# Bias rows written by ScalarE, dense spread of gamma and beta, and the last feed-forward pair by batch

## The reference

```python
# tokens: depthwise conv (3 taps) over time, linear 64 -> 128, biases, layernorm
x_sp    = conv(x, conv_w) + conv_b                 # per channel
x_mixed = einsum('btc,dc->btd', x_t, lin_w) + lin_b + emb.mean(axis=0)
h = (x_mixed - mu) * rsqrt(var + 1e-05) * ln_g + ln_b
# attention on n = layernorm(h): scores in 250 x 250 per batch, scale 1/8
V = softmax(Q K^T / 8) V0 ; the row c0 = argmin(row_sums of batch 0) is set to 0
h = h + V
# feed-forward over the 128 features, weights lower triangular
h = h + (gelu(layernorm(h) @ tril(W1).T + b1) @ tril(W2).T + b2)
```

## Time and profile before

| | us |
|---|---|
| median of three runs | 94.94 (94.71 to 95.37) |
| the profiled execution | 94.69 |
| its span in the trace | 92.9 |
| PE busy | 87.2, 94% of the span |
| DVE busy | 74.4, 80% |
| ACT busy | 69.3, 75% |
| POOL busy | 47.8, 51% |

### The profile page before, as it was taken

One profiled execution on the slowest core, in us unless ns is written; L12 is line 12 of the kernel. 1 busy time (PEld: TensorE's weight loads), 2 busy tenths in 40 slices (PEclk: granted clock), 3 DMA queues, 4 the chain that ended last, 5 costly groups with the idle time before them and its releaser, 6 DMA issues.

```text
span 92.9 us, 2013 instructions
## 1 busy us (share of the span) xinstructions
PE 87.2 (94%) x567; PEld 73.9 (80%) x567; DVE 74.4 (80%) x296; ACT 69.3 (75%) x215; POOL 47.8 (51%) x70
## 2 busy tenths in 40 slices
PE   4999699999999999999999999999999999999940
PEld 1356567789999999999999999999997877787840
DVE  3279997999698998869998895988989688793560
ACT  1666799899999969977889976697758983565200
POOL 7006398676554386539525519703996305791000
PEclk9999999999999999999999999999999999999999
DMA  2896000000000000000000000000000003036565
GB/s 17 213 280 212 0 0 4 4 0 0 7 0 0 0 0 0 7 4 0 0 4 4 0 7 0 0 0 0 0 0 7 0 0 110 0 110 169 162 175 167
DMA packets 3973, 3.86 MB, mean 42 GB/s; under 512 B 429, under 2 KB 3962, under 8 KB 3962
## 3 DMA queue, kind: packets, MB, share of 16 engines
q1 hardware_dynamic: 3610, 3.35, 12.8%
q10 hardware_dynamic: 352, 0.38, 1.5%
HBM read 1.68 MB, written 2.05 MB: 40 GB/s over the span
## 4 chain that ended last, share of the span: by engine, by line
PE 80%; DVE 9%; DMA 5%; issue 1%; SPq 0%; DVEq 0%
PE bank_o L483 15%; PE bank_s L458 15%; PE bank_at L470 8%; PE bank_pv L434 7%; PE bank_pv L443 7%; PE bank_s L518 7%; DMA x_all<-x_dram 5%; PE bank_x L366 4%; PE bank_x L496 4%; PE bank_nt L507 4%; PE bank_pv L507 4%; PE bank_nt L423 4%; DVE hb_all L1078 2%; DVE tap_a L994 1%; DVE xc L1000 1%; PE bank_o L366 1%
## 5 line engine op out<-in xcount | busy, mean ns | idle before, releaser
L483 PE MATMUL bank_o<-pv,at_sb 125*125 125x129 f32 x128 | 16.8, 273 | 0.0
L458 PE MATMUL bank_s<-n1t,pv 128*125 128x250 f32 x64 | 16.1, 374 | 0.0
L483 PEld LDWEIGHTS bank_o<-pv,at_sb 125*125 125x125 f32 x128 | 15.6, 187 | 0.1
L772 ACT ACTIVATE a<-bank_s,neg_max 125x250 f32<-125x250 f32 x32 | 13.4, 482 | 1.0 <-DVE neg_max L1039 1.0
L1039 DVE TENSOR_REDUCE neg_max<-bank_s 125x2 f32<-125x500 f32 x16 | 10.7, 668 | 2.2 <-PE bank_s L458 2.1
L458 PEld LDWEIGHTS bank_s<-n1t,pv 128*125 128x125 f32 x64 | 11.0, 187 | 0.9
L780 ACT ACTIVATE at_sb<-bank_at 125x500 f32<-125x500 f32 x16 | 9.6, 597 | 2.4 <-PE bank_at L470 1.8
L276 POOL TENSOR_TENSOR hb_all<-h_all,rows_sb 125x512 f32<-125x512 f32 x8 | 10.9, 1384 | 0.0
L765 ACT ACTIVATE pv<-bank_pv 128x508 f32<-128x508 f32 x15 | 9.0, 602 | 2.1 <-PE bank_pv L443 2.0
L272 POOL TENSOR_TENSOR h_all<-h_all,rows_sb 125x512 f32<-125x512 f32 x6 | 7.6, 1271 | 5.7 <-DVE h_all L1013 5.7
L1050 DVE SCALAR_TENSOR_TENSOR h_all<-bank_o,rinv_keep,h_all 125x128 f32<-125x128 f32 x32 | 9.8, 346 | 0.6
(11 more groups left out here) (137 smaller groups left out, 183.7 us busy)
## 6 DMA issues: line engine op xcount, KB each, us to landing
out_dram<-hb_all SPq DMA_DIRECT2D x7, 224.0 KB
x_all<-x_dram SPq DMA_DIRECT2D x8, 125.0 KB, 4.9
out_dram<-hb_all SPq DMA_DIRECT2D x2, 112.0 KB
w_sb<-weights_dram SPq DMA_DIRECT2D x1, 192.0 KB, 5.6
rows_sb<-rows_dram ACTq DMA_DIRECT2D x1, 187.5 KB
out_dram<-hb_all SPq DMA_DIRECT2D x6, 26.0 KB
tok_w<-tok_dram ACTq DMA_DIRECT2D x1, 130.0 KB, 3.1
w_sb<-weights_dram SPq DMA_DIRECT2D x1, 128.5 KB, 5.2
```

The source lines that it names most:

```text
L458: last = nc.tensor.matmul(s_ps[b % 2][:, a, :], p_sb(b)[:, a * H:(a + 1) * H], n1t[b % 2][:, :], start=True, stop=True)
L483: last = nc.tensor.matmul(o_ps[:, a, 0:DV], at_sb[:, c, a * H:(a + 1) * H], v_sb(b, c), start=(c == 0), stop=(c == 1))
L772: last = nc.scalar.activation(a_sb[b % 2][:, a, :], s_ps[b % 2][:, a, :], ACT.Exp, bias=neg_max[b % 2][:, a:a + 1])
```

## The change

It has five parts, and the lists of PE, ACT, DVE and POOL are written in a new order around them.

1. **Bias rows.** The bias row is formed on all 128 partitions (`bias_row`), ACT copies it to `cb_sb` (`out_cb`). For pairs 4 to 7 ACT writes it, four times side by side, into the PSUM bank (`write_bias`), and the linear layer is added to that. Pairs 2 and 3 still get it from PE as bfloat16 parts; the split is now four POOL instructions.
2. **gamma and beta.** One row of 1 KB is loaded into a zeroed tile, PE spreads it over 125 partitions (`spread_constants`, 256 columns), ACT copies it (`out_constants`). b2 is loaded and spread by a DMA of SP, behind all x pairs.
3. **First tap of pair 1** goes from DVE to ACT.
4. **Nine dummy matmuls become six.**
5. **Pair 7's feed-forward by batch.** Root, `normalize_2`, `turn_n2`, `out_n2t`, `up`, `gelu`, `down` and `finish` of pair 7 are two turns (j = 7 and 8) of one batch each.

```diff
+        def turn(j):
+            return (j, 0, 4, 2 * j + 2) if j < NP - 1 else (NP - 1, 2 * (j - NP + 1), 2, j + NP)
 @block.sync
...
+            sp.dma_start(b2_sb[:, :], rows[:, 2 * D:3 * D].broadcast_to((H, D))).then_inc(landed_b2, 16)
...
 @block.gpsimd
+            def split_hi():
+                pool.wait_ge(cb_out, 1)
+                pool.tensor_copy(cb_rows[:, :], cb_sb[:, :]).then_inc(cb_hi_ready, 1)
+            def split_rest():
+                pool.wait_ge(cb_hi_ready, 1)
+                pool.tensor_tensor(cb_rest[:, :], cb_sb[0:64, :], cb_rows[0:64, :], ALU.subtract).then_inc(cb_rest_ready, 1)
...
+            pool.memset(rows_raw[:, :], 0.0).then_inc(raw_zeroed, 1)
...
 @block.tensor
             def project_bias(k):
-                before = (0, 0, 1, 0, 4, 6, 10, 12)[k]
...
-                    pe.wait_ge(cb_ready, 3)
-                    if k >= 4:
-                        pe.wait_ge(conv_ready, k + 1)
-                    nc.tensor.matmul(dst, ones_b[:, :], cb_rows[:, :].unsqueeze(1).broadcast_to((C + 1, 4, D)),
+                    pe.wait_ge(cb_ready, 1)
+                    nc.tensor.matmul(dst, shares_b[:, :], cb_rows[:, :].unsqueeze(1).broadcast_to((128, 4, D)),
             def project_half(k, a):
                 pe.wait_ge(conv_ready, k + 1)
+                if k >= 4:
+                    pe.wait_ge(bias_ready, k - 3)
+            def spread_constants():
+                pe.wait_ge(mean_w_ready, 2)
+                pe.wait_ge(landed_rows, 16)
+                nc.tensor.matmul(bank_at[0:H, 0:2 * D], mean_w[:, 0:H], rows_raw[:, :], start=True, stop=True).then_inc(rows_mm, 1)
-            keep_warm(9)
+            keep_warm(6)
+            spread_constants()
...
 @block.scalar
...
-            act.dma_start(rows_sb[:, :], rows.broadcast_to((H, 3 * D))).then_inc(landed_rows, 16)
+            act.wait_ge(raw_zeroed, 1)
+            act.dma_start(rows_raw[0:1, :], rows[:, 0:2 * D]).then_inc(landed_rows, 16)
+            def out_constants():
+                act.wait_ge(rows_mm, 1)
+                nc.scalar.activation(rows_sb[:, :], bank_at[0:H, 0:2 * D], ACT.Copy, scale=float(C)).then_inc(rows_out, 1)
+            def out_cb():
+                act.wait_ge(cb_mm, 1)
+                nc.scalar.activation(cb_sb[:, :], bank_s[0][:, 0:D], ACT.Copy).then_inc(cb_out, 1)
+            def write_bias(k):
+                act.wait_ge(cb_out, 1)
+                act.wait_ge(conv_ready, k + 1)
+                nc.scalar.activation(x_bank(k)[0:H, :].rearrange("p (a d) -> p a d", d=D),
+                                     cb_sb[0:H, :].unsqueeze(1).broadcast_to((H, 4, D)), ACT.Copy).then_inc(bias_ready, 1)
+            out_constants()
+            first_tap(1)
+            first_tap(2)
             squares(0)
+            first_tap(3)
+            out_cb()
             squares(1)
...
```

More of the change, by code:

```diff
@@ L269, in add_beta, with split_low, add_b2 @@
+            def split_low():
+                pool.wait_ge(cb_mid_ready, 1)
+                pool.tensor_tensor(cb_rows[0:32, :], cb_rest[0:32, :], cb_rows[0:32, :], ALU.subtract)\
+                    .then_inc(cb_ready, 1)
             def add_beta(k):
-                pool.wait_ge(landed_rows, 16)
+                pool.wait_ge(rows_out, 1)
                 pool.wait_ge(x_scaled, 2 * k + 2)
                 pool.tensor_tensor(h_tiles[:, k, :, :], h_tiles[:, k, :, :], beta_4, ALU.add).then_inc(h_ready, 1)
-            def add_b2(k):
-                pool.wait_ge(resid_ready, 2 * k + 2)
-                pool.tensor_tensor(hb_all[:, k, :, :], h_tiles[:, k, :, :], b2_4, ALU.add).then_inc(hb_ready, 1)
+            def add_b2(j):
+                k, first, count, batches = turn(j)
+                tiles = slice(first, first + count)
+                pool.wait_ge(landed_b2, 16)
+                pool.wait_ge(resid_ready, batches)
+                pool.tensor_tensor(hb_all[:, k, tiles, :], h_tiles[:, k, tiles, :], b2_4[:, 0:count, :], ALU.add).then_inc(hb_ready, 1)
@@ L494, in turn_n2 @@
                     pe.wait_ge(n2t_ready, j - 1)
-                for n in range(4):
-                    last = nc.tensor.transpose(t2_ps[j % 2][:, n * H:(n + 1) * H], n2[:, j, n, :], ident[0:H, 0:H])
+                k, first, count, _ = turn(j)
+                for n in range(count):
+                    last = nc.tensor.transpose(t2_ps[j % 2][:, n * H:(n + 1) * H], n2[:, k, first + n, :], ident[0:H, 0:H])
                 last.then_inc(t2_mm, 1)
@@ L568, in _ @@
             queries(3)
+            values(3)
+            project_half(5, 0)
             turn_n1(4)
-            values(3)
+            project_half(5, 1)
             attend(0)
@@ L584, in _ @@
             turn_a(3)
+            turn_n1(7)
+            scores(5)
             queries(6)
-            scores(5)
-            project_bias(6)
             values(6)
-            turn_n1(7)
             attend(3)
             turn_a(4)
-            turn_n1(8)
             scores(6)
             queries(7)
+            values(7)
             project_half(6, 0)
-            values(7)
             project_half(6, 1)
+            turn_a(5)
+            turn_n1(8)
             attend(4)
-            turn_a(5)
             scores(7)
+            queries(8)
+            turn_a(6)
+            values(8)
             turn_n1(9)
-            queries(8)
-            values(8)
-            project_bias(7)
+            attend(5)
+            scores(8)
+            queries(9)
             project_half(7, 0)
+            values(9)
             project_half(7, 1)
-            scores(8)
-            attend(5)
-            turn_a(6)
-            queries(9)
             turn_n1(10)
-            values(9)
-            turn_a(7)
             attend(6)
             scores(9)
+            turn_a(7)
             queries(10)
@@ L782, in out_n2t @@
             def out_n2t(j):
+                k, first, count, _ = turn(j)
                 act.wait_ge(t2_mm, j + 1)
-                nc.scalar.activation(n2t[:, j, :], t2_ps[j % 2], ACT.Copy).then_inc(n2t_ready, 1)
+                nc.scalar.activation(n2t[:, k, first * H:(first + count) * H], t2_ps[j % 2][:, 0:count * H], ACT.Copy)\
+                    .then_inc(n2t_ready, 1)
             def gelu(j):
+                k, first, count, _ = turn(j)
                 act.wait_ge(f1_mm, j + 1)
-                nc.scalar.activation(g_sb[:, j, :], f1_ps[j % 2], ACT.Gelu, bias=b1_col).then_inc(gelu_ready, 1)
+                nc.scalar.activation(g_sb[:, k, first * H:(first + count) * H], f1_ps[j % 2][:, 0:count * H], ACT.Gelu, bias=b1_col)\
+                    .then_inc(gelu_ready, 1)
             act.wait_ge(landed_tok, 16)
@@ L816, in _ @@
             out_n1t(0)
+            out_qk(2)
+            squares(6)
             normalize_1(1)
-            spread_rows()
             out_p0()
             first_tap(4)
-            squares(6)
+            out_v0()
             out_n1t(1)
             squares(7)
-            out_v0()
+            spread_rows()
             normalize_1(2)
@@ L905, in _ @@
             out_at(12)
-            out_n2t(0)
+            gelu(0)
+            out_pv(15)
             exps(14)
-            out_pv(15)
             out_at(13)
```

474 lines of the change are left out of this document (228 added, 246 removed).

## The result

Six runs of the changed kernel have a median of 96.00 us, six of the kernel before 94.82; the ratio is 1.012 (95% interval 1.008 to 1.016). The change makes the kernel 1.1 us slower: outside the band of 1% around no change at the median, though the interval reaches into it. One run of the six took 98.6 us and is not in the ratio. The profiled execution took 95.98 (before: 94.69), its span is 94.1 (92.9).

What follows compares the result with a forecast made beforehand. PE was taken to bound the kernel, gapless from 13.50 to 88.26 us, behind a head chained over ACT, POOL and DVE. Terms 0.57 - 0.66 + 0.38 + 0.10 = +0.39 on 94.69 gave 95.1, range 93.7 to 96.6.

Steps and rivals of the forecast that it cites:

- the size of part 1: Bias rows of pairs 4 to 7: PE drops four matmuls, 1.06 us off its gapless stretch.
- the head eats it: Head through pair 4's halves: later queries and PE's waits for ACT cost +0.57, first bias row's 0.40 already taken off.
- nothing happens between 22 and 68 us: From pair 4's halves to the projections' end PE runs without gaps, three bias rows less: -0.66.
- The floor rival: Whole kernel: ACT keeps up and the head is not later; 93.7 to 94.1 us, chance 0.30.
- the order of Gelu and Exp, +0.38: Ahead of the transpose of batch 14's weights: ACT's table change back to Exp makes PE wait, +0.38.
- the third rival: First Gelus: a table change costs more than its load, or ACT is later there; 96.3 to 97.5, chance 0.05.
- the end, +0.10: End, pair 7 by batch: PE waits 0.27 ahead of down(7), the last add follows PE sooner; +0.10, bounds -0.2 and +0.5.
- The -0.17: End: the last add starts 0.22 behind PE's stream instead of 0.39.
- The clock: Head: with fewer dummies the clock stays at 1.2 GHz, all that follows 1.0 to 1.5 late; 96.3, chance 0.17.
- the point of 5.5: Head: the low-clock case decides if the clock rises later than 5.5 us.
- one of my signs that the sum is wrong: Head: the sum is wrong if matmuls behind the dummies still run at the low clock.
- my own mechanism: Whole kernel: gain in the middle and losses at both ends; 95.1, own range 94.3 to 95.9, chance 0.48.

Runs made afterwards that it cites:

- number 3: Changed kernel with ACT's four bias writes undone: PE writes the rows of pairs 4 to 7 from the bfloat16 parts; 97.25 us, ratio 1.023.
- number 12: Changed kernel with number 8's lists, six more tiny memsets at DVE's start and eight dummy matmuls in place of six; 95.39 us, ratio 1.005.
- number 10: Changed kernel with only the first of POOL's four split instructions, the rest of the bias of pairs 2 and 3 left out; ratio 1.008.
- number 5: Changed kernel with the transpose of batch 14's attention weights into another PSUM bank, so it no longer waits for out_at(13); 96.45 us, ratio 1.016.
- number 4: Changed kernel with up(7) one place earlier on PE, ahead of down(6); 96.05 us, ratio 1.012.
- number 9: Changed kernel with six tiny memsets more at DVE's start; 95.69 us, ratio 1.007.
- number 8: Changed kernel with the last part in the order of before, pair 7 still by batch, and out_pv(15) ahead of exps(14); 95.70 us, ratio 1.006.
- number 2: Changed kernel with bias rows of pairs 2 and 3 formed by PE in float32, without POOL's split; 96.86 us, ratio 1.017.
- number 6: Changed kernel with nine dummy matmuls in place of six; 96.49 us, ratio 1.017.
- number 7: Changed kernel with the whole last part on PE, ACT and DVE in the order of before, pair 7 still by batch; 96.21 us, ratio 1.014.
- number 11: Number 7 with nine dummy matmuls; 96.29 us, ratio 1.016.

## Why the prediction was right, and where it was not

**Right: the size of part 1, and that the head eats it.** Of the -1.06 for four rows number 3 confirms 0.88 from the other side. The head came out step by step: squares at 6.83 (7.3 predicted; the loads landed earlier than I took), the first root of the attention's end at 12.50 (12.6), queries of batch 0 at 15.05 (15.05), pair 4's halves at 22.05 (21.98). Squares came 0.5 earlier without moving queries, and that is luck: the first root took POOL from 7.51 to 8.93, 0.4 longer than I took, and three steps of the split 1.3 in place of 1.1, so the two misses cancel. In the chain POOL's two casts, two subtractions and three roots lead to that point. Number 12 closes the ledger: with every later loss repaired, the span equals that of before. The bias rows' gain and the head's loss (0.64, and the 0.40 of the first row) cancel. What bounds the head is only in part the split: without three quarters of it the kernel gains some 0.4, and that not clear of the error (number 10).

**Right: nothing happens between 22 and 68 us.** PE is busy without a gap there while ACT carries 2 us more. The floor rival was right in this stretch and wrong at both ends.

**Wrong in size: the order of Gelu and Exp, +0.38 against +1.03.** I counted load, Exp and signals behind the copy of the values, and took the Exp as the last thing the transpose waits for. It has a second wait: bank_at must be read out by out_at(13), and that copy stands behind exps(14). Number 5 measures this at 0.57 (in the chain it is the 0.49 at 70.30). Without it 0.31 of idle time is left, and 0.15 more for the overlap that PE loses when it starts again (the idle time alone is 0.88, the distance of the starts 1.03): 0.46 by the sum's own terms, where I had 0.38. The tables themselves were as cheap as the row said; the load abuts both neighbours in ACT's timeline of the changed kernel, for the earlier trace rows:

```profile
67.57 0.59 ACT L815 ACTIVATE pv<-bank_pv 128x508 f32<-128x508 f32 x1
68.17 1.28 ACT L822 ACT_TABLE_LOAD   x1
69.47 0.83 ACT L822 ACTIVATE a<-bank_s,neg_max 125x250 f32<-125x250 f32 x2
70.19 0.59 ACT L830 ACTIVATE at_sb<-bank_at 125x500 f32<-125x500 f32 x1
```

The Trainium skill's 2.66 us per switch ("ScalarE: Activation LUTs", "What ACT_TABLE_LOAD costs") is not seen at any of the three: from the end of the copy to the start of the Exp there are 1.31 us. Of the third rival the first half, that a change costs more than its load, is ruled out as a mechanism. Its second half, that ACT is late there by more than I let it, is what came, at 1.03 and not at 1.5 and more.

**Wrong in kind: the end, +0.10 against +0.48 up to the last add.** The wait ahead of down(7) was 0.31 (0.27 predicted), and number 4 shows that taking it away only hands it to down(8), since the Gelu of up(8) is the later one. Two terms were wrong. The -0.17 rested on a wrong reading: PE's stream of before ended at 89.42 and not at 89.14, so the last add already followed it by 0.11, and there was no 0.17 to win. And 0.36 were missed that no engine causes: the stall in DVE's stream, gone with six instructions more (number 9). Nothing in the profile of before shows it.

**The clock: a rival that was true in part of the runs.** In the profiled execution matmuls ran at 1.2 GHz until about 5.8, by the same product at two times:

```profile
4.83 1.08 PE L448 MATMUL bank_x<-emb_c,mean_w 128*125 128x256 f32 x2
...
6.83 0.59 PE L448 MATMUL bank_nt<-emb_c,mean_w 128*125 128x256 f32 x2
```

That is past the point of 5.5 that I named, and matmuls behind the dummies at the low clock were one of my signs that the sum is wrong. The sign was a false one: in number 8 the clock was up from 4.9 on, and its queries of batch 0 start at 15.10, no earlier than the 15.05 here. The profile's own row of the granted clock is of no help: it has its highest digit, 9, in every slice of the first 90 us of these profiles, and only the lengths of the matmuls show the low clock. But of 80 runs of kernels with six dummies 17 took 2.5 to 3.4 us more than the others of their kernel (98.1 to 99.6), and the three profiles of such runs (numbers 2, 5 and 10) show the clock's rise at 13 to 14 us; of 66 runs of the kernel before none did, nor any of 18 with eight or nine. So the risk was right (0.17 given), its price too low (96.3 against 98.6), and it concerns single runs, not the median. The Trainium skill's rule, that the low clock is the default which sustained activity releases ("TensorE: Matmul & The Clock Gate", Part 1), agrees with the rows at the start of every kernel here. Nor is a run-in of nine always enough for a rise at 4.5: in number 6's profile it came at about 6.8.

**In all** the forecast of 95.1 missed 96.0 by 0.9: 0.65 from the second wait of one transpose, 0.52 from the stall and the other steps between PE and the last add, less 0.33 behind the last add, which I had not predicted, and 0.06 from the rest; the kernel came out just beyond the 1% where I had put most of the chance within. 96.0 lies in the range of 93.7 to 96.6, but above the 94.3 to 95.9 of my own mechanism. The room up there was for a low clock that makes the head late; that is not what filled it, and so that the range held is partly luck.

**Open.** What DVE's stall is. POOL has one of the same kind, an idle time of 0.41 to 0.42 put down to issue ahead of one of its adds near 38 us (40.8 in number 5), in the eleven profiles in which POOL has 78 instructions; it is absent in numbers 2 and 10, where POOL has 74 and 75, and in the kernel before with its 70, and six instructions more on DVE don't move it. So both go by the place in their own engine's stream; what happens at that place no run shows.

Also open is what follows the last add. From its end to the end of the profiled execution there are 4.74 us in the kernel before, 4.50 in the changed one and 4.62 in number 9, but 5.66, 5.74, 5.44 and 5.44 in numbers 7, 8, 11 and 12, the four with the last part in the order of before. Most of what these repairs win up to the last add (0.79 to 1.62 us against the changed kernel) is lost there, and it is more than number 12 still loses. No run changes the output transfers or their queues alone, so the cause isn't known.

## What to carry to other kernels

List every semaphore that an instruction waits for, not only the one that brings its data: a buffer's release can stand behind the very instruction that was moved. A table change or a wait is paid only where the other engine has no work beside it, so an order of two engines is moved together or not at all. And work taken off the bounding engine is worth its length only if the head of the chain doesn't get longer by it: here about 1 us came off PE, and small steps of ACT and POOL ahead of the first queries put it back.

## What the runs showed of the hardware

- A stall of 0.36 us ahead of one DVE instruction that has nothing to wait for; it is there in eleven profiles with 290 DVE instructions and goes away when six are added ahead of it.
- A change of ACT's function tables costs its load, 1.28 us, plus 0.01 to 0.02 on each side, in both directions (Exp to Gelu and back).
- TensorE's rise from 1.2 to 2.4 GHz at the start, by the lengths of its matmuls, is not fixed: at 4.5 us (before), 5.8 (changed) and 6.8 (number 6), and at 13 to 14 in three profiles of kernels with six dummies; 17 of 80 runs of such kernels took as much longer as these. The profile's row of the granted clock doesn't show it.
- ACT can write a PSUM bank (125x512 from a 128-column row, repeated), in 0.60 to 0.68 us, and matmuls then add to what it wrote: four such writes replace four matmuls of 0.22.
